# Clearing slots from another queue, and spreading four small copies over four units, in a pipelined attention

## The reference, cut to what matters

```python
qkv = (x @ Wqkv).reshape(b, l, 3, H, DH)          # x is 8 x 512 x 256, H = 16, DH = 16
q = q * cos + rotate_half(q) * sin                # k likewise
scores = jnp.einsum('bqhd,bkhd->bhqk', q, k) * scale
attn = jax.nn.softmax(scores, axis=-1)
out = jnp.einsum('bhqk,bkhd->bqhd', attn, v).reshape(b, l, d) @ Wo
```

## Time and profile before

| what | value |
|---|---|
| time, median of 3 runs | 1306.05 us (1303.21 to 1308.11) |
| profiled execution, its own time | 1302.63 us |
| its span, first to last instruction | 1300.8 us |
| TensorE busy | 1179.3 us, 91% |
| VectorE busy | 954.4 us, 73% |
| ScalarE busy | 898.6 us, 69% |
| mean granted TensorE clock | 0.959 of 2.4 GHz |

### The profile page before, as it was taken

One profiled execution on the slowest core, in us unless ns is written; L12 is line 12 of the kernel. 1 busy time (PEld: TensorE's weight loads), 2 busy tenths in 40 slices (PEclk: granted clock), 3 DMA queues, 4 the chain that ended last, 5 costly groups with the idle time before them and its releaser, 6 DMA issues. The chain is left out here.

```text
span 1300.8 us, 26963 instructions
## 1 busy us (share of the span) xinstructions
PE 1179.3 (91%) x8416; PEld 864.4 (66%) x8416; DVE 954.4 (73%) x1871; ACT 898.6 (69%) x1970; POOL 580.1 (45%) x589
## 2 busy tenths in 40 slices
PE   2588989898999998987999969999999999999997
PEld 2333333333333332236899969999999999999897
DVE  6377877787878887837776648877777777777596
ACT  1457877687878776665654427777777877777687
POOL 5232323232313210004547755666666666666773
PEclk8579999999999999998899989999999999999999
DMA  9734343434334433345122237777777777776373
GB/s 291 185 67 89 80 86 76 86 82 88 81 70 82 78 79 78 68 136 176 34 82 95 90 126 230 252 246 242 238 238 237 250 251 251 244 238 219 107 214 120
DMA packets 264654, 194.52 MB, mean 150 GB/s; under 512 B 156352, under 2 KB 247488, under 8 KB 264576
## 3 DMA queue, kind: packets, MB, share of 16 engines
q1 hardware_dynamic: 247568, 164.45, 44.7%
q0 software_dynamic: 6816, 18.75, 4.0%
q10 hardware_dynamic: 10192, 10.38, 2.6%
HBM read 122.06 MB, written 37.52 MB: 123 GB/s over the span
## 5 line engine op out<-in xcount | busy, mean ns | idle before, releaser
L545 DVE TENSOR_REDUCE att_mx<-att_psA 128x1 f32<-128x512 f32 x512 | 329.5, 679 | 98.2 <-PE att_psA L342 96.7
L453 ACT ACTIVATE pre_acc<-att_psB 128x512 f32<-128x512 f32 x512 | 283.3, 599 | 122.0 <-PE att_psB L352 117.2
L352 PE MATMUL att_psB<-att_qk 128*128 128x512 bf16 x512 | 197.5, 389 | 30.0 <-DMA att_qk<-att_mrow 28.1
L342 PE MATMUL att_psA<-att_qk 96*128 96x512 bf16 x512 | 200.3, 395 | 9.0 <-DVE att_mx L545 2.9
L1643 ACT ACTIVATE exp_psU<-exp_psU,ew_b 128x256 f32<-128x256 f32 x312 | 126.7, 446 | 103.6 <-PE exp_psU L1600 103.6
L1694 DVE CAST exp_hh<-exp_psU 128x512 fp32r<-128x512 f32 x156 | 107.9, 692 | 101.8 <-ACT exp_psU L1643 101.8
L1583 PE MATMUL exp_psD<-exp_w2h,exp_hh 128*128 128x256 f32 x624 | 176.1, 282 | 0.0
L1598 PE MATMUL exp_psU<-exp_xh,exp_w1h 128*128 128x256 f32 x624 | 174.1, 279 | 1.4 <-DVE exp_xl L1685 1.4
L1599 PE MATMUL exp_psU<-exp_xl,exp_w1h 128*128 128x256 f32 x624 | 173.7, 278 | 0.0
L1600 PE MATMUL exp_psU<-exp_xh,exp_w1l 128*128 128x256 f32 x624 | 173.5, 278 | 0.0
L1585 PE MATMUL exp_psD<-exp_w2h,exp_hl 128*128 128x256 f32 x624 | 172.7, 277 | 0.0
(11 more groups left out here) (214 smaller groups left out, 2917.6 us busy)
## 6 DMA issues: line engine op xcount, KB each, us to landing
ew_w<-ew SPq DMA_DIRECT2D x40, 1024.0 KB, 5.7
exp_w<-ew SPq DMA_DIRECT2D x38, 1024.0 KB, 4.9
slots_x<-pre_acc ACTq DMA_DIRECT2D x13, 780.0 KB, 10.5
pre_spare<-slots_x SPq DMA_DIRECT2D x39, 260.0 KB, 4.2
out_g<-rows_y SPq DMA_DIRECT2D x32, 256.0 KB, 4.3
ew_b<-eb SPq DMA_DIRECT2D x39, 128.0 KB
pre_spare<-xT SPq DMA_DIRECT2D x8, 512.0 KB, 4.3
att_qk<-att_stack SPq DMA_TRANSPOSE x256, 2.5
```

The costliest lines, as they stand in the source:

```text
L342: pe.matmul(psA[A_BANK[n % U]][:, :], r[:, 0, qt * P:(qt + 1) * P], r[:, 1, :], start=True, stop=True).then_inc(s_amm, 1)
L352: pe.matmul(psB[B_BANK[n % U]][:, :], r[:, 1, kt * P:(kt + 1) * P], r[:, 0, :], start=True, stop=True).then_inc(s_bmm, 1)
L453: act.activation(prob[:, n % PR, :], psB[B_BANK[n % U]][:, :], ACT.Exp, scale=SCALE).then_inc(s_exp, 1)
L545: dve.reduce_max(mx[:, g % 2, n % U:n % U + 1], psA[A_BANK[n % U]][:, :], AX_X).then_inc(s_max, 1)
```

## The change

Three things are edited. The 13 clearing DMAs leave ScalarE's start; SyncE issues one at the end of each of the periods 0 to 12, behind `place_max`. The four instructions of `spread` go into units 0, 1, 2 and 3, one each, each behind the exponential of its unit (and the last behind `copy_out`, which is in unit 3 too). Small steps change units: `turn_out` 5 to 7, the norm of the output 5 and 6 to 8 and 9, `turn_max` 10 to 11, `copy_max` 9 to 10, `piece_1` 6 to 7. The block of zeros that GpSimd fills at the start shrinks from 2560 to 1792 columns.

```diff
-    PROJECT_QK, ROPE, COPY_OUT, TURN_OUT, NORM_OUT = (0, 1), (1, 2, 3), 3, 5, (5, 6)
-    PROJECT_V, COPY_V, SPLIT_MAX, TURN_MAX, COPY_MAX = 13, 13, 8, 10, 9
-    PIECE_1, PIECE_2, SPREAD, SPLIT_X = 6, 10, 0, 12
+    PROJECT_QK, ROPE, COPY_OUT, TURN_OUT, NORM_OUT = (0, 1), (1, 2, 3), 3, 7, (8, 9)
+    PROJECT_V, COPY_V, SPLIT_MAX, TURN_MAX, COPY_MAX = 13, 13, 8, 11, 10
+    PIECE_1, PIECE_2, SPREAD, SPLIT_X = 7, 10, (0, 1, 2, 3), 12
...
-        zero = norm.acc[:, 0:10, :].rearrange("p t d -> p (t d)")
+        zero = norm.acc[:, 0:7, :].rearrange("p t d -> p (t d)")
...
                 if valid(p + 1, NG):
                     place_max(p + 1, it)
+                if valid(p, CHUNKS):
+                    if p == 0:
+                        sp.wait_ge(s_blank, 16)
+                    sp.dma_start(slots[p], blank).then_inc(s_zero, 16)
...
+                if part == 0:
+                    wait(act, it, s_qsp, tile + 1, 1)
+                    act.activation(q[:, :, 1:3, :], q[:, :, 0:1, :].to_broadcast([P, H, 2, DH]), ACT.Copy)
...
+                else:
+                    act.activation(k[:, :, 1, :], k[:, :, 4, :], ACT.Copy).then_inc(s_stk, 1)
...
-            act.wait_ge(s_blank, 16)
-            for c in range(CHUNKS):
-                act.dma_start(slots[c], blank).then_inc(s_zero, 16)
...
-                    if u == SPREAD and valid(p + QK_LEAD - 1, NT * B):
-                        spread(p + QK_LEAD - 1, it)
+                    if u in SPREAD and valid(p + QK_LEAD - 1, NT * B):
+                        spread(p + QK_LEAD - 1, SPREAD.index(u), it)
```

More of the change, by code:

```diff
@@ L467, in copy_v, with spread @@
                 act.activation(V[:, b % 2, t, :, 0:DH], bank[:, 0:D].rearrange("p (h d) -> p h d", d=DH), ACT.Copy).then_inc(s_vev, 1)
-            def spread(tile, it):
+            def spread(tile, part, it):
                 b, t = tile // NT, tile % NT
                 q, k = (stack[:, b % 2, t, i, :, 0:KR].rearrange("p h (m d) -> p h m d", d=DH) for i in range(2))
[L473 to L477, removed]
+                if part == 0:
+                    wait(act, it, s_qsp, tile + 1, 1)
+                    act.activation(q[:, :, 1:3, :], q[:, :, 0:1, :].to_broadcast([P, H, 2, DH]), ACT.Copy)
+                elif part == 1:
+                    act.activation(k[:, :, 3:6:2, :], k[:, :, 0:1, :].to_broadcast([P, H, 2, DH]), ACT.Copy)
+                elif part == 2:
+                    act.activation(q[:, :, 3, :], q[:, :, 4, :], ACT.Copy)
+                else:
+                    act.activation(k[:, :, 1, :], k[:, :, 4, :], ACT.Copy).then_inc(s_stk, 1)
             def piece_1(tile, it):
```

## The result

| | before | changed |
|---|---|---|
| median | 1305.07 us (1303.21 to 1308.11, 4 runs) | 1322.54 us (1320.23 to 1323.82, 4 runs) |
| profiled execution, span | 1302.63, 1300.8 us | 1323.82, 1322.0 us |
| mean granted TensorE clock | 0.959 | 0.952 |
| first transposes; first exponential | 42.53; 78.33 us | 31.86; 67.60 us |
| last exponential | 573.94 us | 596.66 us |

The ratio is 1.0131 [1.0106, 1.0156]: slower by 17.5 us, 7.5 us above the time forecast and inside the range. The attention started 10.7 us earlier and ended 22.7 us later.

What follows compares the result with a forecast made beforehand. Bounds: TensorE in plain periods, SyncE's queue where sequences begin, ScalarE's clearing issues at the start. Terms -10.65 + 0 + 18.8 + 3.4 - 2.5 = +9.05 on 1302.63 gave 1311.7; with the median 3.4 higher, 1315 us, range 1300 to 1328.

Steps and rivals of the forecast that it cites:

- The start: Without 13 clearing issues on ScalarE, SyncE's first transposes and the first columns come earlier: -10.65 us, bounds 9 to 12.5.
- The clearing on SyncE: Thirteen clearing issues behind the maxima in SyncE's queue delay nothing that is wanted soon: 0 us, bounds 0 and 26.6.
- the third rival: Clearing packets get ahead of the maxima, each delaying them in full: 26.6 us more, 1342 us; chance 0.05.
- The four units: Last copy ends 3.0 us later in five sequence beginnings and 1.9 in two, delaying the maxima: +18.8 us, bounds 13 and 22.
- The clock: TensorE's half-clock dips after waits at all seven beginnings, 1.45 us each, less 1 us: +3.4 us, bounds 0 and 8.
- with waits twice as long: Clock step: with TensorE's waits doubled, all seven beginnings are counted as dipping, at 1.45 us each.
- The other units: Moved small steps end `turn_out`'s rotation waits; 24 plain periods gain 0.1 us each: -2.5 us, bounds -6.9 and +10.
- The sum: Whole kernel: all five terms added, +9.05 us on the profiled 1302.63 us, giving 1311.7; forecast median 1315 us.
- a hidden delay: ScalarE reaches its fourth exponential sooner, so the last copy is under 0.9 us later: 1293 or 1289 us; chance 0.12.
- the draw: Copies' delay passes on at 15.8 us, but TensorE gets all rotation waits: 1304 us, 1308 with the clock; chance 0.23.

Runs made afterwards that it cites:

- run 1: Kernel before with only the 13 clearing DMAs moved from ScalarE's start to SyncE, one a period: 1296.9 us against 1304.77, ratio 0.9952.
- run 8: run 6 with eight clearings issued in SyncE's idle start and five in periods 2, 6, ... 18: 1275.43 us, ratio 0.9779.
- run 10: run 8 and run 9 together (eight clearings in SyncE's idle start, load of x behind the maxima): 1268.47 us against 1303.76, ratio 0.9737.
- run 2: Kernel before with only the four spread copies put into units 0 to 3: 1326.9 us, ratio 1.0182.
- run 4: Changed kernel with all four copies back in unit 0: 1296.72 us, ratio 0.9943.
- run 3: Kernel before with only the small steps moved (output turn and norm, turning and copy of the maxima, first piece): 1305.3 us, ratio 1.0014.
- Run 5: Changed kernel with the last copy in unit 6 in place of unit 3: 1329.59 us against 1305.87, ratio 1.0177.
- run 7: run 6 with the small steps back in their old units: 1279.98 us, ratio 0.9833.
- run 6: Changed kernel with the four copies in units 14 and 15 of the period before, two in each: 1278.68 us, ratio 0.9806.
- run 9: run 6 with the load of x issued behind the maxima in place of ahead: 1271.21 us, ratio 0.9742.

## Why the prediction was right, and which terms were off

**The start, -10.65 forecast, -10.7 found.** GpSimd's last rest became the bound, SyncE followed at 31.86 against a forecast 31.88, and run 1 shows the part as a gain. The maxima stayed the last thing there: they were issued at 63.91 in place of 74.63, and the first exponential came at 67.60 in place of 78.33. The Trainium skill says of the time that an issue takes on its sequencer ("DMA: Bandwidth & Descriptors", section "Issuing engines are not separate DMA queues") that it is usually small beside the DMA. Here it was not: 13 large DMAs in a row held ScalarE for 26.64 us.

**The clearing on SyncE, 0 forecast, some 3 to 4 us found, with a wide error.** Its issue is 0.58 us there, not 2.05, the lower of the two figures that I named. Run 1 leans to a cost of 3 to 4 us in all, 1.3 to 7.6 by its interval. Moving the issues to other places gave 2.0 us (run 8) and 2.7 us (run 10) by the medians, 3.7 and 0.7 by the ratios, and none of it is beyond its error. That it costs nothing isn't shown, then, nor where the cost lies. The 26.6 us of the third rival are excluded by run 1, which is faster than before.

**The four units, +18.8 forecast, +20.9 found in the seven beginnings.** The last copy came 2.9 to 3.0 us later in five and 1.95 in two (forecast 3.0 and 1.9), 18.6 together. The rest goes with longer issue of the eight transposes: 3.0 us more over the seven, most of it in period 1 (11.56 us against 10.48 before) and period 17 (11.73 against 10.38). Its cause is open. The late copy was the step that decided the sign, and runs 2 and 4 show it alone.

**The clock, +3.4 forecast, +8.1 found in the periods behind; this term was mis-sized.** I counted three new dips at the old size, 1.45 us each, less 1. The three beginnings that had escaped (periods 2, 14 and 22 behind them) cost 1.25, 1.8 and 2.7 us, 5.7 together; two old dips that grew to twice their length (behind periods 5 and 17) cost 1.8 more, and period 30 has the rest. That it is the clock can be checked: in the periods behind the beginnings TensorE is busy for 31.1 us at the lower level, against 13.0 before, and half of the difference is 9.0 us. The step that failed is "with waits twice as long" at an unchanged 2.90 us of half clock: the windows show 6.40 us of waiting followed by 5.3 us at 0.50. Period 29's +1.5 has such a dip as well. Part of the term is chance: with waits of about 3 us the dips behind the seven beginnings are four in the profiles of before and of run 4, five in run 3 and six in run 1, so the profile of before is one with few. Run 5 says that the cost doesn't go on growing: waits of up to 8.0 us leave the second column where it was, with 30.4 us at the lower level.

**The other units, -2.5 forecast, 0 found.** The rotation wait went, and a wait for the norm came in front of `turn_max`; I had not looked at that row of VectorE. The maxima, which hang on the same `turn_max`, now come just in time, as the prediction had it. TensorE's weight load for the first columns of period 8, changed and before:

```profile
205.84 0.10 PEld L356 LDWEIGHTS att_psB<-att_qk 128*128 128x128 bf16 x1 [0.30 <-DMA att_qk<-att_mrow]
```

```profile
206.25 0.10 PEld L352 LDWEIGHTS att_psB<-att_qk 128*128 128x128 bf16 x1
```

The maxima landed at 205.79 for columns at 205.88, 0.09 us to spare; before, they landed at 205.80 for columns at 206.46, 0.66. (The 0.6 and 1.15 us in what was expected of run 7 are counted to the first exponential, about half a microsecond behind the columns.) The matmuls lose no pace by it: those columns start 0.22 us behind the matmul ahead of them in both kernels. Seven plain periods have 0.1 us less in all, and run 3 puts the whole between -0.9 and +4.7. What sets a plain period once the rotation wait is gone no run isolates.

**The sum, +9.05 forecast, +17.5 found by medians.** By the profiled executions it is +21.2. Of the 12 us between, the clock and its period 29 hold 6, the small units 2.5 and the copies 2. Periods 0, 4, ... 28 have 2.9, part of which may be the clearing, and 1.5 come back after the attention. All of these terms were forecast too low. Of the rivals, a hidden delay falls with run 2 (the fourth exponential does wait for TensorE), and the draw with runs 2 and 3: of the rotation waits a plain period gave back about 0.06 us.

## What to carry to other kernels

A long strip of issue on one engine and a late signal on another can sit in the same change; price each on the engine that waits for it, and try them apart, since here one part gained 6 to 8 us and another lost 22. When a copy releases a queue that is full to its end, look for an earlier place for it and not for a smoother one: the same four copies, a few units earlier, turned a ratio of 1.0131 into 0.981. And when a small wait is removed, read the next two rows on the engine that is waited for, not only the next one on the path.

## What the hardware showed that I had not expected

The issue of a 780 KB clearing takes 0.58 us on SyncE alone, and 2.05 us each where 13 stand in a row on ScalarE; they land in 4.4 us (the changed kernel's row above), not in the 10.5 us of before:

```profile
slots_x<-pre_acc ACTq DMA_DIRECT2D x13, 780.0 KB, 10.5
```

Three small DMAs land later behind a 512 KB load in their queue: 3.0 us (median, changed kernel, period 5; 2.9 in run 6) against 1.7 us with the load behind them in run 9. The rows of issues, first of the changed kernel, then of run 9:

```profile
att_qk<-att_mrow SPq DMA_DIRECT2D x3, 4.0 KB, 3.0
```

```profile
att_qk<-att_mrow SPq DMA_DIRECT2D x3, 4.0 KB, 1.7
```

This agrees with the Trainium skill, "DMA: Bandwidth & Descriptors", section "Queues, rings and completion order", by which descriptors are consumed in ring order: SyncE's load and maxima share its queue. The 1.3 us are this case's number. No run here tells the order in the queue from a sharing of the DMA engines.

In period 5 a standstill of TensorE twice as long was followed by almost twice as long a stretch at the lower clock level, 6.40 and 5.3 us against 3.10 and 2.90. The two don't always go together: in the changed kernel a wait of 4.57 us behind period 9 was followed by 3.4 us of work at that level, and one of 4.00 us behind period 21 by 6.2 us.
